# A recurrence on GpSimd in 32 double steps, with VectorE preparing and completing it

## The reference, cut to what matters

```
h = table[ids]                                    # 64 sequences x 128 tokens x 256
h = h + block(layernorm(h))
h = h + int8_linear(layernorm(h))                 # one scale for all of x

mixer of the block, on x = rms(layernorm(h)):
  zgate, u, B, C, dt = split(x @ in_proj.T)       # 512, 512, 16, 16, 8
  u, B, C = silu(causal_conv4(u, B, C))
  B, C = B / |B|, C / |C|                         # per token, over 16
  d = softplus(dt + bias)                         # per token and head (8 heads)
  for t in range(128):                            # state z, y: head x 64 x 16
      z = (z + d*(u*B - A*y)) / (1 + d*d*A)
      y = y + d*z
      out = sum_n(y * C)
  y = (out + D*u) * silu(zgate);  x + y @ out_proj.T
MLP: x + gelu(rms(x) @ fc1.T) @ fc2.T             # 256 -> 1024 -> 256
```

## Time and profile before

| what | us |
|---|---|
| median of 3 runs | 1336.01 (1335.78 to 1336.26) |
| profiled execution, its own time | 1340.35 |
| its span, first to last instruction | 1338.0 |
| TensorE busy in the span | 1130.1 (84%) |
| VectorE | 1078.9 (81%) |
| GpSimd | 821.7 (61%) |
| ScalarE | 786.6 (59%) |

### The profile page before, as it was taken

The page is one execution under the profiler, slowest core; times in us unless marked ns, Lnnn a source line. Parts: engine busy times, 40 slices in busy tenths (PEclk is TensorE's granted clock), DMA queues, the critical chain, the costliest instruction groups (busy, mean ns, idle before and its releaser), DMA issues. The chain is left out here.

```text
span 1338.0 us, 24711 instructions
## 1 busy us (share of the span) xinstructions
PE 1130.1 (84%) x7206; PEld 750.8 (56%) x7206; DVE 1078.9 (81%) x1770; ACT 786.6 (59%) x1275; POOL 821.7 (61%) x2278
## 2 busy tenths in 40 slices
PE   3981034589999999999999999999999999997957
PEld 1550012457575757575666666575757566756634
DVE  5988959959797979797978888787979796976078
ACT  4666546374748484747484756656574748452367
POOL 8881020576777878787878777878787877760000
PEclk9999997699999999999999999999999999998879
DMA  9999801010101010101010000000010101000015
GB/s 366 406 409 415 335 11 29 15 35 3 36 2 36 2 36 0 36 2 34 7 30 13 23 18 19 18 19 20 16 31 5 36 1 37 2 18 1 0 59 193
DMA packets 62274, 92.77 MB, mean 69 GB/s; under 512 B 9117, under 2 KB 55026, under 8 KB 57826
## 3 DMA queue, kind: packets, MB, share of 16 engines
q1 hardware_dynamic: 58530, 82.10, 17.2%
q0 software_dynamic: 3072, 8.39, 1.6%
q10 hardware_dynamic: 576, 1.31, 0.3%
HBM read 81.29 MB, written 10.49 MB: 69 GB/s over the span
## 5 line engine op out<-in xcount | busy, mean ns | idle before, releaser
L771 POOL TENSOR_TENSOR stp<-Gs,X 128x32 f32<-128x32 f32 x960 | 289.6, 302 | 182.1 <-ACT X L746 110.4
L773 POOL TENSOR_TENSOR Gs<-Gs,stp 128x32 f32<-128x32 f32 x960 | 283.4, 295 | 75.8
L1151 PE MATMUL bank<-w_fc,gl 128*128 128x256 f32 x1024 | 244.4, 382 | 5.5 <-ACT gl L1142 5.5
L1132 PE MATMUL bank<-mT,w_fc 128*128 128x512 f32 x512 | 240.4, 603 | 1.4 <-ACT mT L1112 1.4
L626 PE MATMUL bank<-xT,w_in 128*128 128x512 f32 x512 | 233.8, 600 | 0.1
L1151 PEld LDWEIGHTS bank<-w_fc,gl 128*128 128x128 f32 x1024 | 189.8, 190 | 69.3 <-issue 31.2
L921 ACT ACTIVATE uT<-bank,cols 128x512 f32<-128x512 f32 x64 | 47.9, 775 | 220.4 <-DVE sz L1055 175.2
L626 PEld LDWEIGHTS bank<-xT,w_in 128*128 128x128 f32 x512 | 93.7, 190 | 99.0 <-issue 93.0
L1132 PEld LDWEIGHTS bank<-mT,w_fc 128*128 128x128 f32 x512 | 96.3, 193 | 88.5 <-issue 82.7
L935 DVE SCALAR_TENSOR_TENSOR uT<-bank,cols,uT 128x500 f32<-128x500 f32 (+1 forms) x192 | 133.4, 733 | 2.7 <-ACT uT L921 0.4
L344 DVE TENSOR_TENSOR peak<-ring,peak 128x1536 f32<-128x1536 f32 (+2 forms) x67 | 115.3, 1721 | 7.8 <-ACT ring L246 6.2
(11 more groups left out here) (198 smaller groups left out, 1845.6 us busy)
## 6 DMA issues: line engine op xcount, KB each, us to landing
ring<-in_table SPq DMA_DIRECT2D x31, 1536.0 KB
d_rep<-d_rows SPq DMA_DIRECT2D x128, 64.0 KB, 2.7
out<-res SPq DMA_DIRECT2D x16, 512.0 KB, 2.9
b_rep<-bc_rows SPq DMA_DIRECT2D x128, 32.0 KB, 1.8
c_rep<-bc_rows SPq DMA_DIRECT2D x128, 32.0 KB, 1.8
w_fc<-in_w_fc SPq DMA_DIRECT2D x2, 1024.0 KB, 8.5
ring<-in_table SPq DMA_DIRECT2D x2, 768.0 KB
w_in<-in_w_in ACTq DMA_DIRECT2D x1, 1088.0 KB
```

Source lines behind the costliest of these rows:

```text
L771: pool.tensor_tensor(stp[:], Gs[:, t, ::-1, :], X2[:, t, :, :], ALU.mult).then_inc(rec.sem, 1)
L773: pool.tensor_tensor(Gs[:, t + 1, :, :], Gs[:, t, :, :], stp[:], ALU.add).then_inc(rec.sem, 1)
L1132: last = pe.matmul(pj[n % 4][:, :], w_fc1[:, k, n * P:(n + 1) * P], mT[:, k, :], start=(k == 0), stop=(k == KD - 1))
L1151: last = pe.matmul(sbk[j // 2][:, (j % 2) * D:(j % 2 + 1) * D], gl[n % LEAD][:, j * LEN:(j + 1) * LEN], w_fc2[:, n, :], start=False, stop= ...
```

## The change

Only the second stage is touched.

- `pool_recurrence` does two steps in one: G[2k+2] = (1 - x0 x1) G[2k] + (X2[2k] + X2[2k+1]) * swap(G[2k]), three operations (two multiplies that don't depend on each other, one add) and 32 such pairs. The rms factors come after pair 21 (`RMS_PAIR`).
- `dve_pairs` (new) makes, for the whole group, the factor `pr` = 1 - x0 x1 (512 elements per partition, two operations) and the sums, which overwrite the odd X2 (1024 elements).
- `dve_between` (new) fills the odd states behind the recurrence with two operations of 1024 elements; rm is its scratch. Its signal `states` takes the place of `rec` where squares, keys and X2's rewriting waited for the recurrence.
- bk of a group moves a turn ahead, since the odd X2 are lost after `dve_pairs`: `dve_next` is bk, then `dve_pairs`, and stands between keys and inverse of p. The normed B, C (`dve_bc`) move from the end of the turn to in front of `dve_between` (in turn 1 behind the keys).
- bc_rows and d_rows lie in DRAM as (row, sequence, time), so that a copied row is 2 KB in one piece; for this each is stored with four DMAs, one per sequence.
- ScalarE's squares, and all four X2 copies at once, come after the third gelu (before: squares after the first, X2 after the third and the fourth).
- xT's first half may be overwritten after the first of the two accumulating products of z's last tile (`z_left`), and the small projection waits for each half of xT by itself.
- In turn 1 the quantisation of g+1 stands behind the reciprocals.

```diff
-RMS_STEP = 47
+RMS_PAIR = 21
+PAIRS_T = CL // 2
...
         def act_rows_T(act, g):
-            if since(g):
-
-                act.wait_ge(z_mm.sem, z_mm.at(g - 1))
             for k in range(KD):
+                if since(g) and k == 0:
+                    act.wait_ge(z_left.sem, z_left.at(g - 1))
+                elif since(g):
+                    act.wait_ge(z_mm.sem, z_mm.at(g - 1))
...
-            sp.dma_start(d_rows.rearrange("j r t -> (j r) t"), dd[:]).then_inc(d_stored.sem, 16)
+            for j in range(G):
+                sp.dma_start(d_rows[:, j, :], dd[SMALL * j:SMALL * j + HEADS, :]).then_inc(d_stored.sem, 16)
...
-            sp.dma_start(bc_rows.rearrange("j r t -> (j r) t"), bcd[:]).then_inc(bc_stored.sem, 16)
+            for j in range(G):
+                sp.dma_start(bc_rows[:, j, :], bcd[SMALL * j:SMALL * (j + 1), :]).then_inc(bc_stored.sem, 16)
...
+        def dve_pairs(dve, g):
+            dve.wait_ge(x_ready.sem, x_ready.at(g))
+            dve.scalar_tensor_tensor(pr[:], X2[:, 0::2, 0, :], -1.0, X2[:, 1::2, 0, :], ALU.mult, ALU.mult) \
+                .then_inc(paired.sem, 1)
+            dve.wait_ge(paired.sem, paired.at(g - 1, 1))
+            dve.tensor_scalar(pr[:], pr[:], 1.0, None, ALU.add).then_inc(paired.sem, 1)
+            dve.tensor_tensor(X2[:, 1::2, :, :], X2[:, 0::2, :, :], X2[:, 1::2, :, :], ALU.add).then_inc(paired.sem, 1)
...
+            for k in steps:
+                if k:
+                    pool.wait_ge(rec.sem, rec.at(g - 1, 3 * k))
+                pool.tensor_tensor(stp[:, 0], pr[:, k:k + 1, :].to_broadcast([P, 2, LANES]), Gs[:, 2 * k, :, :],
+                                   ALU.mult).then_inc(rec.sem, 1)
+                pool.tensor_tensor(stp[:, 1], X2[:, 2 * k + 1, :, :], Gs[:, 2 * k, ::-1, :], ALU.mult) \
+                    .then_inc(rec.sem, 1)
+                pool.wait_ge(rec.sem, rec.at(g - 1, 3 * k + 2))
+                pool.tensor_tensor(Gs[:, 2 * k + 2, :, :], stp[:, 0], stp[:, 1], ALU.add).then_inc(rec.sem, 1)
...
+        def dve_between(dve, g):
+            dve.wait_ge(rec.sem, rec.at(g - 1))
+            odd = rm[:].rearrange("p t l -> p (t l)").rearrange("p (n a l) -> p n a l", a=2, l=LANES)
+            dve.tensor_tensor(odd, X2[:, 0::2, :, :], Gs[:, 0:CL:2, ::-1, :], ALU.mult).then_inc(filled.sem, 1)
+            dve.wait_ge(filled.sem, filled.at(g - 1))
+            dve.tensor_tensor(Gs[:, 1:CL:2, :, :], Gs[:, 0:CL:2, :, :], odd, ALU.add).then_inc(states.sem, 1)
...
+        def dve_next(dve, g):
+            for hg in range(HG):
+                dve_bk(dve, g, hg)
+            if since(g):
+                dve_pairs(dve, g)
...
 (VectorE's turn)
-                if second:
-                    for hg in range(HG):
-                        dve_bk(dve, p, hg)
-                if first:
-                    dve_d(dve, g)
+                if first and not filling:
+                    dve_d(dve, g)
+                if first and second and third:
+                    dve_bc(dve, g)
+                if second and since(p):
+                    dve_between(dve, p)
                 if second:
                     dve_keys(dve, p)
+                if first and second and not third:
+                    dve_bc(dve, g)
+                if first and second:
+                    dve_next(dve, g)
+                if second:
                     dve_inverse(dve, p, 0)
...
-                if first and second:
-                    dve_bc(dve, g)
```

More of the change, by code:

```diff
@@ L493, in build @@
         bk_ready = signal("bk_ready", HG)
-        rec = signal("rec", 2 * CL)
+        rec = signal("rec", 3 * PAIRS_T)
+        paired = signal("paired", 3)
+        filled = signal("filled", 1)
+        states = signal("states", 1)
         pair = sem("pair")
@@ L505, in build @@
         z_mm = signal("z_mm", UT)
+        z_left = signal("z_left", 1)
         z_ready = signal("z_ready", UT)
@@ L634, in pe_small @@
                 for k in range(KD):
+                    if part == 0:
+                        pe.wait_ge(xT_ready.sem, xT_ready.at(g, k + 1))
                     for j in range(G):
@@ L760, in pool_recurrence @@
         def pool_recurrence(pool, g, steps):
             if steps[0] == 0:
[L763 to L773, removed]
+                pool.wait_ge(kq.sem, kq.at(g - 1, 10))
@@ L851, in dve_keys @@
         def dve_keys(dve, g):
-            dve.wait_ge(rec.sem, rec.at(g))
+            dve.wait_ge(states.sem, states.at(g))
             dve.wait_ge(bk_ready.sem, bk_ready.at(g))
@@ L951, in pe_z @@
             pe.wait_ge(u_cv.sem, u_cv.at(g, u_convolved(f)))
-            project(pe, pj[f][:, :], f * P, (f + 1) * P, z_mm.sem)
+            if f < UT - 1:
+                project(pe, pj[f][:, :], f * P, (f + 1) * P, z_mm.sem)
+                return
+            for k in range(KD):
+                last = pe.matmul(pj[f][:, :], w_in[:, k, f * P:(f + 1) * P], xT[:, k, :],
+                                 start=(k == 0), stop=(k == KD - 1))
+                if k == 0:
+                    last.then_inc(z_left.sem, 1)
+            last.then_inc(z_mm.sem, 1)
         def act_silu_z(act, g, tiles):
@@ L1309, in turn @@
                         act_gelu(act, m, n)
-                    if second and n == 0:
+                    if second and n == LEAD - 1:
                         act_squares(act, p)
[L1312 to L1315, removed]
+                    if first and n == LEAD - 1:
+                        act_rep(act, g, (0, 1))
                     if second and n == 5:
@@ L1340, in turn @@
                 p, m = g - 1, g - 2
-                if nxt:
+                filling = second and not third
+                if nxt and not filling:
                     dve_quantise(dve, g + 1)
@@ L1344, in turn @@
                     dve_conv_small(dve, g)
-                if second:
-                    for hg in range(HG):
-                        dve_bk(dve, p, hg)
-                if first:
+                if first and filling:
                     dve_d(dve, g)
+                if first and not filling:
[4 more added lines that the diff above has]
+                    dve_between(dve, p)
                 if second:
                     dve_keys(dve, p)
+                if first and second and not third:
[3 more added lines that the diff above has]
+                if second:
                     dve_inverse(dve, p, 0)
@@ L1356, in turn @@
                         dve_queries(dve, p, 1)
+                if nxt and filling:
+                    dve_quantise(dve, g + 1)
                 if nxt:
@@ L1406, in turn @@
                 if first and second:
[L1407 removed]
+                    pool_recurrence(pool, g, range(0, PAIRS_T // 2))
                 if nxt:
```

34 lines of the change are left out of this document (19 added, 15 removed).

## The result

The change makes the kernel slower: 1518.19 us (median of 4 runs, 1516.66 to 1519.97) against 1335.89, a ratio of 1.1369 (95% interval 1.1355 to 1.1383), +182 us. The forecast was 1510 within 1468 to 1535. The profiled execution took 1519.97 us, its span 1518.2, granted clock 0.887 where it had been 0.970.

A forecast was written before the change was run, and what follows sets the result against it. A ring of VectorE and TensorE, the fullest engine, bounds the turn. Thirteen steady turns +153, turn 1 +10.5 and turn 15 +10.9 sum to 174 us: profiled 1340.35 becomes 1514, median 4.3 lower, 1510, range 1468 to 1535.

The forecast's parts named there:

- The ring: VectorE and TensorE tie each steady turn; work added between VectorE's convolution and masks lengthens it: masks 9.7 us later.
- step 5: VectorE's bk behind the keys waits for SyncE's copies of B: stall of 4.2 us, bounds 0 and 5.4.
- Step 6: Four stores for one: lead 2.9 us for 1.55, copies of d land some 1.4 us later, cost 0.
- step 3: VectorE fills odd states, keys start 1.0 us later; TensorE idles 1 to 2 us in the second MLP product, cost 0.
- Step 8: GpSimd's 96 recurrence operations take 36 us, 28 if independent products overlap; hidden, with GpSimd waiting at the rms.
- Step 9: Earlier rms, xT's half release and split wait remove TensorE's 0.36 us: -0.5 us a turn, bounds 0 and 1.
- Step 10: TensorE idles 6 us ahead of the scan's products, then runs slow: +2.6 us a turn, bounds 0 and 5.2.
- Turn 1: VectorE stands 8 us for B, masks come about 14.5 later, TensorE's wait and slow clock give -4: sum +10.5 us.
- A: Rival: TensorE's clock stays full, or falls too late to matter: 1474 us, chance 0.15.
- B: Rival: the copies of B don't hold VectorE up, TensorE idles too little for a slow clock: 1411 us, chance 0.05.
- C: Rival: GpSimd becomes the bound, each operation 0.5 us, filling waits about 4 us per turn: 1566 us, chance 0.04.
- D: Rival: VectorE's additions all fall into waits and TensorE closes its 1.5 us in 14 turns: 1315 us, chance 0.02.

The follow-up runs named there:

- e1: Changed kernel with the copies of B waiting only for the old bk, those of C still for the eleventh key signal: 1457.27 us, ratio 1.085.
- e4: Kernel before, recurrence in 64 steps untouched, with B, C norms ahead of the keys and the next group's bk behind them: 1449.98 us, ratio 1.0817.
- e3: Changed kernel with B's copies waiting for the old bk alone and six unread products ahead of the first scan products: 1415.93 us, ratio 1.0556.
- e2: Changed kernel with unread products in TensorE's holes, four ahead of the first scores, six ahead of the first scan products: 1470.39 us, ratio 1.0952.
- e5: Changed kernel with bk made from the copied d at its old place, and B, C norms at the turn's end: 1370.13 us, ratio 1.0263.
- e6: Changed kernel with bk from copied d, norms at the turn's end, factors and filling on GpSimd, rms after pair 29: 1347.86 us, ratio 1.0069.

## Why the prediction was right

**The ring.** Right in kind: everything that VectorE got between convolution and masks came back in the turn, 40.5 - 31.1 = +9.4 us for +9.7 forecast. The parts: keys +1.2 for +1.0 (the filling's hand-over of 0.24 was not in the sum), stall 3.91 for 4.2, bk and factors 4.3 (856.91 to 861.18) for 4.5. e1 shows the stall's cause, e4 that bk and norms alone bring it.

**The stall of step 5** was worked out from an issue train and a landing, and e1, which takes away only the wait ahead of the train, brings the masks 50 us forward over 13 turns, and 61 us in all with what TensorE's clock gives back.

**Step 6** erred on the copies of d: they began 2.2 us behind the first store, not 2.9, and the longer rows landed 2.0 us after the issue, not 2.7, so X2 was done sooner, the fourth gelu was not late, and the hole of step 3 in the MLP didn't come up. Without effect on the sum. What the prediction took from the Trainium skill (DMA: Bandwidth & Descriptors, Anatomy of one DMA — SWDGE (gpsimd) path), that longer rows don't shorten the landing, is borne out by B's copies, 1.8 us before and after, and not by those of d, 2.7 and 2.0; the section is on copies that GpSimd issues, and these are SyncE's.

**Step 8.** Right, between its two figures: a double step is 0.87 us where VectorE leaves GpSimd alone, and all take some 32 us, for 28 or 36. GpSimd waits for the sums of squares. Step 9 gave up to 0.9 for 0.5.

**Step 10 was mis-sized.** It forecast one hole of 6 us and a loss of 2.6 us. There were two holes with slow work between, the first ahead of the scores (4.00 us, which the step named but didn't count as one that lowers the clock), so TensorE was at 1.2 GHz from the scores on and until into u's projection. The loss is 4.1 us a turn by e3's rows, 4.2 by e2, inside the step's bounds of 0 and 5.2. The products that it priced were not the ones either: the first scan products did cost 1.7 us more (3.68 us), but the output products took 7.07 us as before, and the second scores (3.69 us for 2.01) and u's first projection (4.78 for 3.70) slowed in their place. With ring and step 9 this gives the turn: 9.4 - 0.9 + 4.1 = 12.6, for the forecast's 11.8, 10 us more in 13 turns. The Trainium skill's figure of under 1% for the ramp (TensorE: Matmul & The Clock Gate, What's actually happening) would have allowed 13 us; e2 alone got back 48.

**Turn 1** was dearer in the forecast (+10.5) than on the chip (+7.75). The stall was 7.93 us for 8, but its masks came 13.0 us later, not 14.5: the 1.46 us that they had waited for the scores were named in the sum and not taken off. Behind the masks the turn saved 5.2 us for the forecast's 4. Turn 15 and after: +8.5 for +10.9; there TensorE idled only 0.39 us ahead of the scan products and was at 1.00 in them, so the 2.6 us for the clock didn't come. These two errors take back about half of step 10's: 174 forecast in the sum, 180 in the spans. That the forecast lies within 8 us is to that extent luck.

Of the rivals, A's premise (a clock that stays) didn't occur by itself; e2 and e3 had to bring it about. B is e1, which shows its 1411 too low: without the stall the hole and the slow clock stay, and B's 2 us "less than needed for a slow clock" had no row behind it (in e5 the slow clock followed idles of 2.23 and 2.75 us in some turns). C is excluded by GpSimd's waits. D's 1315 needs turns of some 62.4 us, which only e6's first turns reach (62.3 to 63.0), and its reasoning was right in one point, that TensorE with 62.3 us is next.

## What to carry to other kernels

An engine that ends late is worth relieving only by what its consumer waits for it, here 3.3 us of a turn, and what the relief needs from the consumer has to fit into that. Before an operation is moved, look at which wait it fills now and what its inputs wait for at the new place: bk cost nothing in a wait of 3 us and 6 us behind the keys, 4 of them because one semaphore wait guarded B with C. If the helper has time to spare, as GpSimd had here, let it do the preparation too, but in pieces short enough for the neighbour that it locks out.

## What the runs showed of the hardware

- In the changed kernel TensorE idled 4.00 us and then ran at 0.50 from the scores at 789.11 to within u's projection, which begins at 806.14, with an idle of 2.40 us between. Unread products in the holes gave 4.2 us a turn back. With nearly the same idles in every turn the loss went round in three sizes: 33.7, 37.5 and 36.0 us from masks to convolution, for 31.9 at the full clock.
- Idles of 2.75 to 2.80 us between the same products lowered the clock in three turns of e5 and not in the others with the same idle, 4.9 us of a turn apart; an idle of 2.23 us lowered it for some 3 us.
- GpSimd's operations over 1024 elements took 2.35 us, over 512 1.27, over 256 0.73, over 32 0.25; of two independent ones the second starts 0.21 us behind the first, a dependent one 0.33.
- VectorE's four quantising operations beside the two of 2.35 us took 5.64 us for 1.38. A convolution that reads a bank took 1.12 us beside such an operation, as without it.
- A copy to 32 partitions landed after 2.0 us with rows of 2 KB and after 2.7 with four pieces of 512 B; B's copies to 16 partitions after 1.8 with either.
